# A decoder on one core: cross tails packed before their transpose, the first keys' turned probabilities copied by VectorE, and the row sums of self units 0 to 6 sent through DRAM

## What is computed

```python
def attn_block(xq, ctx, Wq, Wk, Wv, Wo, bo, pe_q, pe_k, mask):
    q, k, v = heads(xq @ Wq), heads(ctx @ Wk), heads(ctx @ Wv)      # 8 heads of 64
    q, k = apply_rope(q * 64 ** -0.5, pe_q), apply_rope(k, pe_k)
    a = jax.nn.softmax(jnp.einsum('bhid,bhjd->bhij', q, k), axis=-1)
    return merge(jnp.einsum('bhij,bhjd->bhid', a, v)) @ Wo + bo
for l in range(4):
    h = rmsnorm(x, sg[l]); x = attn_block(h, h, ...) + x            # 512 keys
    h = rmsnorm(x, cg[l]); x = attn_block(h, chunked_seq, ...) + x  # 154 keys
    h = rmsnorm(x, fg[l]); x = gelu(h @ fW1[l] + fb1[l]) @ fW2[l] + fb2[l] + x
```

## Time and profile before

| | |
|---|---|
| median of 3 runs | 1397.63 us (1396.97 to 1398.51) |
| the profiled execution | 1397.06 us |
| its span in the trace | 1395.0 us |
| the four layers | about 76 to 1010 us |
| a layer's self part; its cross part | 128 us; 76 us (layer 0) |
| PE, ACT, DVE, POOL busy | 90%, 53%, 51%, 29% |

### The profile page before, as it was taken

How to read it: one execution, slowest core, us unless ns; L and a number is a source line. 1 busy time by engine, 2 the same in 40 slices (tenths; PEclk the granted TensorE clock), 3 DMA queues, 4 the chain that set the end, 5 groups by cost and what they waited for, 6 DMA issues and landing times.

```text
span 1395.0 us, 21171 instructions
## 1 busy us (share of the span) xinstructions
PE 1255.1 (90%) x7630; PEld 754.9 (54%) x7630; DVE 710.3 (51%) x2061; ACT 742.3 (53%) x1897; POOL 399.2 (29%) x379
## 2 busy tenths in 40 slices
PE   4499998989999898999989899998759995898898
PEld 2244555554455464445556445465449993454687
DVE  6665554356555435555543555644334115675454
ACT  1176666637666654765664576665323444364332
POOL 1343332254332316324321633422220101110100
PEclk8599999999999999999999999999969998899799
DMA  4000000010000001000000000000011100000010
GB/s 142 0 1 0 24 1 9 23 29 2 0 24 8 2 24 29 1 1 23 9 24 8 16 1 1 16 2 1 1 56 31 38 25 0 1 1 1 9 35 24
DMA packets 27096, 22.49 MB, mean 16 GB/s; under 512 B 4342, under 2 KB 22131, under 8 KB 26995
## 3 DMA queue, kind: packets, MB, share of 16 engines
q1 hardware_dynamic: 26995, 21.14, 5.2%
HBM read 20.60 MB, written 0.52 MB: 15 GB/s over the span
## 4 chain that ended last, share of the span: by engine, by line
PE 83%; DVE 9%; POOL 3%; ACT 2%; issue 1%; DMA 0%; SPq 0%; DVEq 0%; POOLq 0%
PE bank L1455 13%; PE bank L1414 10%; PE bank L1433 8%; PE bank L1474 7%; PE bank L1486 6%; PE bank L1466 4%; PE bank L1631 4%; PE bank L1430 4%; PE bank L1407 3%; PE bank L1479 3%; PE bank L1569 2%; PE bank L1571 2%; PE bank L1570 2%; PE bank L1847 2%; PE bank L1538 1%; PE bank L1735 1%
## 5 line engine op out<-in xcount | busy, mean ns | idle before, releaser
L798 DVE CUSTOM_DVE_ANT_0 bank<-bank,maskrow 128x512 f32<-128x512 f32 x256 | 172.3, 715 | 151.5 <-PE bank L1414 151.3
L1179 ACT ACTIVATE probs<-bank,tops 128x512 f32<-128x512 f32 x256 | 174.3, 685 | 128.0 <-DVE tops L798 127.9
L612 POOL TENSOR_TENSOR rot<-rot,sin 128x512 f32<-128x512 f32 (+1 forms) x112 | 134.3, 1199 | 376.2 <-DVE rot L787 376.2
L1191 ACT ACTIVATE KA<-bank 128x512 f32<-128x512 f32 x256 | 139.1, 600 | 31.8 <-PE bank L1433 31.8
L1414 PE MATMUL bank<-QA 64*128 64x512 f32 x512 | 146.6, 653 | 7.7 <-DVE rot L787 7.0
L1433 PEld LDWEIGHTS bank<-ident,probs 128*128 128x128 f32 x1024 | 116.8, 141 | 54.4 <-issue 45.5
L1433 PE MATMUL bank<-ident,probs 128*128 128x128 f32 x1024 | 134.7, 274 | 2.3 <-ACT Vs L1156 2.3
L1455 PE MATMUL bank<-KA,Vs 128*64 128x512 f32 x512 | 135.4, 615 | 0.0
L1175 ACT ACTIVATE probs<-bank,tops 128x154 f32<-128x154 f32 x256 | 95.5, 383 | 57.1 <-DVE tops L795 56.6
L614 POOL TENSOR_TENSOR QA<-rot 128x512 f32<-128x512 f32 x96 | 121.8, 1269 | 7.5
L786 DVE TENSOR_TENSOR rot<-bank,cos 128x512 f32<-128x512 f32 (+1 forms) x112 | 73.8, 659 | 74.3 <-PE bank L1474 55.6
(11 more groups left out here) (250 smaller groups left out, 2191.5 us busy)
## 6 DMA issues: line engine op xcount, KB each, us to landing
f<-in_fW SPq DMA_DIRECT2D x8, 256.0 KB, 3.1
Vc<-in_wup SPq DMA_DIRECT2D x8, 192.0 KB, 2.5
wk<-in_sWk SPq DMA_DIRECT2D x4, 256.0 KB, 2.8
wq<-in_sWq SPq DMA_DIRECT2D x4, 256.0 KB, 3.2
wv<-in_sWv SPq DMA_DIRECT2D x4, 256.0 KB, 4.1
wo<-in_sWo SPq DMA_DIRECT2D x4, 256.0 KB, 3.7
ck<-in_cWk SPq DMA_DIRECT2D x4, 256.0 KB, 2.7
cv<-in_cWv SPq DMA_DIRECT2D x4, 256.0 KB, 3.1
```

Source lines behind the costliest of these rows:

```text
L612: g.tensor_tensor(turned, turned, tab, ALU.mult).then_inc(q.pool_step, 1)
L798: v.tensor_tensor_reduce(bank[i][:, :], bank[i][:, :], maskrow[:, u.b * S:(u.b + 1) * S], -SCALE, 3.0e38, ALU.add, ALU.min, tops[:, g % 4, ...
L1179: c.activation(to, bank[i][:, :], ACT.Exp, bias=tops[:, g % 4, e, 0:1], scale=-1.0, accum_out=sums[:, n, k, e:e + 1]).then_inc(q.probs_rea ...
L1191: c.activation(turned_self(u)[:, half, :, k * P:(k + 1) * P], bank[4 + half][:, :].rearrange("p (c t) -> p c t", t=P), ACT.Copy).then_inc( ...
```

## The change

Units 0 to 6 of each layer (28 in all) are no longer spread by PE. `recs` is laid out by head and query block; SP stores a unit's 128x8 reciprocals to a DRAM tensor so that the queries of a head lie in a row (single words of 4 bytes), waits until they have landed, and loads each head's row of 512 into 64 partitions of `recT`. `normalise` waits for these loads. Units 7 to 15 are spread as before. SP's weight loads are put at given steps between the sends.

In cross steps POOL (`pack_tails`) copies the 26 last keys of both heads and both query blocks of step s+2 into `xpad`, 32 columns for each of the four, ahead of the pieces of step s. PE turns `xpad` once instead of four blocks of 26. The turned tails then lie in bank 5 on four groups of 32 rows (by query block, then head), and ACT moves them with two copies of 64x128, one for each query block, so that head 0 is on rows 0 to 31 of `KA` and head 1 on rows 32 to 63. For the weighing each head has a row group of its own, so the tail values are made twice, on rows 0 to 31 and 32 to 63 (`last_values`). DVE, not ACT, copies bank 4 (the first 128 keys) in cross steps. `xpad` is zeroed at the start of the program instead of ahead of the last attention. The diff, cut:

```diff
@@ -79,6 +79,15 @@
+NEAR = tuple(range(7, 16))
+def rows_sent(n):
+    return sum(i % (2 * UNITS) not in NEAR for i in range(n + 1))
@@ -107,12 +116,12 @@
-                roped = True
+                roped = not x.unit.cross
...
-                    spread=[units[i] for i, t in SPREAD.items() if t == s],
+                    spread=[units[i] for i, t in SPREAD.items() if t == s and i in NEAR],
@@ -239,8 +250,8 @@
-        sums = sb("sums", [P, 4, TB, 2])
-        recs = sb("recs", [P, 4, TB, 2])
+        sums = sb("sums", [P, 4, 2, TB])
+        recs = sb("recs", [P, 4, 2, TB])
@@ -518,8 +534,21 @@
-            for l in range(LAYERS):
-                if l:
+            def send_rows(u):
+                i = u.n % 4
+                sp.wait_ge(q.rec_ready, u.n + 1)
+                sp.dma_start(dram_r[i].rearrange("e t p -> p (e t)"), recs[:, i, :, :].rearrange("p e t -> p (e t)"),
+                             allow_slow_non_contiguous=True).then_inc(q.rec_out, 16)
+                sp.wait_ge(q.rec_out, 16 * rows_sent(u.n))
+                if u.n >= 2:
+                    sp.wait_ge(q.heads_ready, u.n - 1)
+                for e in range(2):
+                    sp.dma_start(recT[e * DH:e * DH + DH, u.n % 2, :],
+                                 dram_r[i, e].rearrange("t p -> (t p)").partition_broadcast(DH)).then_inc(q.spread_in, 16)
+            def loads(l, s):
+                if l and s == 3:
@@ -527,19 +556,30 @@
-                if l + 1 < LAYERS:
+                if s == 34:
...
-                    load_self(l + 1)
+                    if l + 1 < LAYERS:
+                        load_self(l + 1)
+                    else:
+                        load_expert0(0, 0)
+                if l + 1 < LAYERS and s == 36:
...
+                if l + 1 < LAYERS and s == 42:
...
-                else:
-                    sp.wait_ge(q.roped, made["q", l, 1, PAIRS - 1])
-                    sp.wait_ge(q.v_ready, made["v", l, 1, TB - 1])
-                    load_expert0(0, 0)
+            for step in ORDER.steps:
+                if step.unit:
+                    last = step.before and step.before.unit
+                    if last and step.k == 0 and last.n % (2 * UNITS) not in NEAR:
+                        send_rows(last)
+                    loads(step.unit.l, step.g % 48)
+                for p in step.pieces:
+                    if p.what == "out" and 2 * UNITS - 1 not in NEAR:
+                        send_rows(p.step.unit)
@@ -632,8 +673,23 @@
+            def pack_tails(step):
+                g_, r = step.g, 2 * (step.g % 4)
+                pool.wait_ge(q.probs_ready, 2 * g_ + 2)
+                if see.n.get("tails_ready", 0) == 0:
+                    pool.wait_ge(q.xpad_zero, 1)
+                else:
+                    pool.wait_ge(q.turned_full, 2 * g_ - 2)
+                see.expect(q.tails_ready)
+                for t in range(2):
+                    ins = g.tensor_copy(xpad[:, g_ % 2, 2 * t:2 * t + 2, 0:C2], ring[:, r:r + 2, t * C + P:t * C + C])
+                ins.then_inc(q.tails_ready, 1)
...
+                    if step.after and step.after.unit.cross:
+                        pack_tails(step.after)
@@ -800,14 +855,10 @@
-                dve.wait_ge(q.turned_full, 2 * step.g + 2)
-                if u.cross:
-                    w = slice(k * 2 * P, (k + 1) * 2 * P)
-                    v.tensor_copy(turned_cross(u)[0:C2, 1, :, w],
-                                  bank[5][0:C2, :].rearrange("p (e t) -> p e t", e=2)).then_inc(q.turned_dve, 1)
-                else:
-                    v.tensor_copy(turned_self(u)[:, 1, :, k * P:(k + 1) * P],
-                                  bank[5][:, :].rearrange("p (c t) -> p c t", t=P)).then_inc(q.turned_dve, 1)
+                dve.wait_ge(q.turned_full, 2 * step.g + 1)
+                w = slice(k * 2 * P, (k + 1) * 2 * P)
+                v.tensor_copy(turned_cross(u)[:, 0, :, w],
+                              bank[4][:, :].rearrange("p (e t) -> p e t", e=2)).then_inc(q.turned_dve, 1)
@@ -817,7 +868,10 @@
-                dve.wait_ge(q.spread_ready, u.n + 1)
+                if u.n % (2 * UNITS) in NEAR:
+                    dve.wait_ge(q.spread_ready, u.n + 1 - rows_sent(u.n))
+                else:
+                    dve.wait_ge(q.spread_in, 32 * rows_sent(u.n))
@@ -1173,26 +1227,26 @@
-                                           accum_out=sums[:, n, 2 * k + t, e:e + 1])
+                                           accum_out=sums[:, n, e, 2 * k + t:2 * k + t + 1])
...
-                                 accum_out=sums[:, n, k, e:e + 1]).then_inc(q.probs_ready, 1)
+                                 accum_out=sums[:, n, e, k:k + 1]).then_inc(q.probs_ready, 1)
...
-                if u.cross:
-                    n = C2 if half else P
-                    w = slice(k * 2 * P, (k + 1) * 2 * P)
-                    c.activation(turned_cross(u)[0:n, half, :, w], bank[4 + half][0:n, :].rearrange("p (e t) -> p e t", e=2),
-                                 ACT.Copy).then_inc(q.turned_act, 1)
+                if u.cross and half:
+                    for t in range(2):
+                        ins = c.activation(turned_cross(u)[0:2 * 32, 1, 0, (2 * k + t) * P:(2 * k + t + 1) * P],
+                                           bank[5][2 * 32 * t:2 * 32 * t + 2 * 32, 0:P], ACT.Copy)
+                    ins.then_inc(q.turned_act, 1)
...
-                act.wait_ge(q.spread_full, u.n + 1)
+                act.wait_ge(q.spread_full, u.n + 1 - rows_sent(u.n))
@@ -1218,9 +1272,9 @@
-                        turned_out(step, 0)
...
-                            turned_out(step, 1)
+                            turned_out(step, 0)
+                        turned_out(step, 1)
@@ -1422,17 +1476,19 @@
-                if u.cross:
-                    n, c0 = (C2, P) if half else (P, 0)
+                if u.cross and half:
+                    pe.wait_ge(q.tails_ready, see.next(q.tails_ready))
+                    ins = turn(bank[5][:, 0:P], xpad[:, g % 2, :, :].rearrange("p j c -> p (j c)"), ident[:, :])
+                elif u.cross:
...
-                            o = bank[4 + half][0:n, (2 * e + t) * P:(2 * e + t + 1) * P]
-                            ins = turn(o, ring[:, r + e, t * C + c0:t * C + c0 + n], ident[:, :])
+                            o = bank[4][:, (2 * e + t) * P:(2 * e + t + 1) * P]
+                            ins = turn(o, ring[:, r + e, t * C:t * C + P], ident[:, :])
...
-                lend([4 + half], q.turned_dve if half and step.dve else q.turned_act)
+                lend([4 + half], q.turned_dve if step.dve and not half else q.turned_act)
@@ -1447,9 +1503,10 @@
-                    if u.cross:
-                        n = C2 if k else P
-                        vals, src = Vc[0:n, 2 * u.b + k, w], turned_cross(u)[0:n, k, e, :]
+                    if u.cross and k:
+                        vals, src = Vc[32 * e:32 * e + 32, 2 * u.b + 1, w], turned_cross(u)[32 * e:32 * e + 32, 1, 0, :]
+                    elif u.cross:
+                        vals, src = Vc[:, 2 * u.b, w], turned_cross(u)[:, 0, e, :]
@@ -1477,6 +1534,14 @@
+                lend([i], q.v_ready)
+            def last_values(i, src, w):
+                free(i)
+                for e in range(2):
+                    ins = mm(bank[i][32 * e:32 * e + 32, :], src, w[:, :], start=True, stop=True)
+                ins.then_inc(q.v_full, 1)
@@ -1518,7 +1583,10 @@
-                    value_tile(i, ctxT[:, c0:c0 + (C2 if j % 2 else P)], cv)
+                    if j % 2:
+                        last_values(i, ctxT[:, c0:c0 + 32], cv)
+                    else:
+                        value_tile(i, ctxT[:, c0:c0 + P], cv)
```

12 lines of the change are left out of this document (9 added, 3 removed).

## The result

| | before | changed |
|---|---|---|
| median | 1397.45 us (4 runs, 1396.97 to 1398.51) | 1378.51 us (4 runs, 1378.25 to 1380.55) |
| ratio, 95% interval | | 0.9866 [0.9854, 0.9878] |
| the profiled execution; its span | 1397.06; 1395.0 us | 1378.32; 1376.6 us |
| predicted | | 1357, range 1346 to 1376 |

The account below looks back on a forecast made before the run. PE, busy 90% of the span, was taken to bound the kernel. Spreads 24.4 plus packed tails 15.9, with the DRAM path hidden at 0, made 40.3 off 1397.06: 1357 us, range 1346 to 1376.

Parts of the forecast that it names:

- The failed step: Way through DRAM for units 0 to 6: issue, words, landing and loads take 7.9 us, hidden, costing 0.
- The cover: Time from unit 1's reciprocals until someone waits for the DRAM path: 13.0 us for DVE, 14.7 for PE.
- Rival D: DRAM path comes late: at 17.0 us, 2.3 beyond PE's 14.7, 28 times, 64 us, giving 1421; chance 0.12.
- B: Cross part gives nothing because POOL and DVE, with more work, take over there: 1372.7 us; chance 0.14.
- A: The forecast itself, 1350 to 1364 us; chance 0.62.
- The page's rule: Store's 64 words per engine at 0.2 us each, 12.8 us, path 17.6: 81 us of stalls, 1438.
- Spreads, 24.4: Self units 0 to 6: 28 spreads removed from PE at 0.87 us each, 24.4 us, all on the path.
- Packed tails, 15.9: Cross steps: three fewer transposes save 0.37 us a step, 5.9 a layer; 4.0 arrives, 15.9 in four layers.
- (a): Steps 34 and 44: the spread waits 0.7 for DVE's reciprocals, so 0.37 gained in each is lost, -0.74 per layer.
- (c): Step 38: POOL packs tails before cq1.1's rotation sum, so step 40's scores come 0.45 late; -1.2 per layer.
- E: Tiles of 32 rows and 64 columns do not run side by side: 40 us more, 1397; chance 0.05.
- The copy to DVE, 0: Cross steps: copying the first keys on DVE, 0.69 for ACT's 0.60, adds 11 us to DVE; put at 0.

Follow-up runs that it names:

- second to fourth runs: The changed kernel, unaltered, measured three more times in later comparisons: 1362.8, 1364.7 and 1363.1 us.
- doubled words: Changed kernel with the 1024 words stored twice, to two DRAM tensors, both waited for: 1618.7 us, ratio 1.1585.
- the transposed store: Changed kernel with reciprocals transposed by DVE in 32x32 blocks and stored as 128 runs of 128 bytes: 1357.7 us, ratio 0.9716.

## Why the prediction was wrong

**The failed step** is "1.2 + 0.8 + 2.3 + 0.8 + 2.8 = 7.9 us: hidden, 0". Its terms 0.8 + 2.3 for the store's words and landing measured 8.7 to 11.4. The fast end was taken from rows of other work: 13 ns a packet, which is even less here (7), and the landing of a store of 256 KB in long runs. Neither row shows what a landing of neighbouring words costs, and the prediction chose the fast end on the strength of a packet row, though the packets were never the question. The loads were taken as independent of the store, at 2.8; in the changed kernel they landed in 2.7 to 6.5, late where the words were reported early, and the two together came to 13.0 to 13.7 in the mean. The issue took 0.38 for 1.2. With the store in runs the same loads land in 2.9 (median) and the kernel takes 1356.8 to 1357.7.

**The cover** was sized on unit 1 (13.0 for DVE, 14.7 for PE) and taken for all 28. The 14.7 is added up wrongly by a little: 120.83 - 0.69 - 0.87 - 104.30 = 14.97. Where nothing is late (the run with runs of 32 bytes), normalise starts 14.2 us behind the reciprocals in unit 0, 13.0 in units 1 to 3, 15.7 and 14.9 in units 4 and 5, and 11.9 in unit 6, and unit 6 has 13.0 until PE waits. In the second to fourth runs most of the loss, 4.9 to 6.1 us, is there.

**Rival D** was the right mechanism, with its place (normalise, then bank 6) and its price confirmed by doubled words; it lay at the start of its range, paths of 13.8 to 15.2 and not 17, so it halved the gain and did not reach break-even. It was weighted 0.12, and the range ended at B with 0.1 us of lateness, so a D between 14.7 and 16.1 was left out; that is why 1378.5 fell outside. The three later runs of the same kernel, 1362.8 to 1364.7, lie inside the range, two of them inside A's. That would have been luck, since the path is not hidden there either: DVE waits 16.7 to 21.7 us for `recT` in them.

**The page's rule** (the Trainium skill, DMA: Bandwidth & Descriptors, Specifications: a read-modify-write under 512 B; my estimate from it 12.8 us, path 17.6) came nearer for this store than my own term, and not for its reason: the same 1024 words 64 bytes apart, all under 512 B too, lag 2.8, and 128 runs of 32 bytes 1.5. The Trainium skill (DMA: Bandwidth & Descriptors, Anatomy of one DMA, written for transfers that GpSimd issues) also says that the semaphore update can't go out until the last byte is confirmed landed in the target memory, and puts most of some 2 us down to this. In unit 0 it is over 9 us from the last packet (89.25 at the latest) to SP's next instruction (99.05), so the figure does not hold for these words, and no run here sees inside that time.

**Spreads, 24.4:** right. With a store that lands early, first `up` of layer 3 comes at 952.43 for 989.21, 36.8 less, of which the cross parts are 12.1 and the rest 24.7.

**Packed tails, 15.9:** measured alone 15.0 in all but only 12.1 in the cross parts, to which the 15.9 had been put. The missing 3.8 are made up in part by a gain outside the layers that was not forecast: in the trace with the transposed store the last layer's first `up` comes 36.8 earlier and the end of the span 39.2. Where those 2.4 come from is open; with them 40.3 looks met. Turning saves 0.33 a step, not 0.37 (64 x 0.04 = 2.6 us of the gap). (a) is there: the spread's wait for reciprocals is 1.0 where it was 0.7. (c) was right in mechanism and near in size, 0.85 a layer measured for 1.2. Not foreseen: 0.34 a layer in step 39, where the tail values, made by PE earlier than before, wait for ACT's copy of `recT`, and 0.2 in step 46, where a weighing waits for normalise. POOL's two copies take 0.39, as taken.

**B** (nothing from the cross part) falls with the tails alone, and **E** (no 32x64 tiles side by side) too: the tail's weighing is 1.07 us for four tiles in the changed kernel, not 2.

```profile
267.98 1.07 PE L1512 MATMUL bank<-KA,Vc 32*64 32x512 f32 x4
```

The copy to DVE, 0: right. The stages behind the layers kept their times within 2.4 us (403.4 to 405.8 from the last layer's first `up` to the end).
